# Second attention: one reciprocal for the row sums of two rounds, and block transposes four rounds behind their scores

## What is computed

```python
q = (q_c @ w_qb).reshape(b, s, NH, QK).transpose(0, 2, 1, 3)      # NH 32, QK 192
...
scores = jnp.einsum('bhqd,bhkd->bhqk', query, key_s) * scaling
attn = jax.nn.softmax(scores, axis=-1)
out = jnp.einsum('bhqk,bhkd->bhqd', attn, v)
out = out.transpose(0, 2, 1, 3).reshape(b, s, NH * VD)
return out @ w_o
```

## Time and profile before

| | |
|---|---|
| Median of 3 runs | 1026.47 us (1021.14 to 1027.76) |
| The profiled execution | 1023.77 us, its span 1021.9 us |
| Mean granted TensorE clock | 0.934 of full speed |
| The second attention | about 390 to 955 us of the span |
| TensorE busy | 849.0 us (83%) |
| VectorE busy | 764.2 us (75%) |
| ScalarE busy | 535.6 us (52%) |
| POOL busy | 520.7 us (51%) |
| Row maxima, L1351 | 256, 171.7 us; VectorE idle before them 36.1 us |
| Transposes, L1366 | 256, 178.6 us |

### The profile page before, as it was taken

How to read it: one execution, slowest core, us unless ns; L and a number is a source line. 1 busy time by engine, 2 the same in 40 slices (tenths; PEclk the granted TensorE clock), 3 DMA queues, 4 the chain that set the end, 5 groups by cost and what they waited for, 6 DMA issues and landing times. The chain is left out here.

```text
span 1021.9 us, 15116 instructions
## 1 busy us (share of the span) xinstructions
PE 849.0 (83%) x4552; PEld 563.1 (55%) x4552; DVE 764.2 (75%) x1588; ACT 535.6 (52%) x1142; POOL 520.7 (51%) x449
## 2 busy tenths in 40 slices
PE   5678886599978965799999999997999999985476
PEld 1667675477767743355555555564555555643145
DVE  1759998745535525999999999999999999982453
ACT  2267874623213743665666666564666665662143
POOL 2034342012110004888888888886888888872013
PEclk9979998599987986999999999998999999998779
DMA  9430000700023770455555555553555555555101
GB/s 328 159 129 2 1 2 1 276 23 1 1 82 126 246 227 0 111 132 126 130 130 129 128 132 131 126 131 93 129 128 132 128 130 129 127 130 118 56 11 72
DMA packets 73105, 112.29 MB, mean 110 GB/s; under 512 B 18816, under 2 KB 23936, under 8 KB 72768
## 3 DMA queue, kind: packets, MB, share of 16 engines
q1 hardware_dynamic: 60736, 94.54, 33.8%
q10 hardware_dynamic: 12288, 16.79, 6.9%
HBM read 42.06 MB, written 2.10 MB: 43 GB/s over the span
## 5 line engine op out<-in xcount | busy, mean ns | idle before, releaser
L1351 DVE TENSOR_REDUCE nmax<-bank 128x1 f32<-128x512 f32 x256 | 171.7, 671 | 36.1 <-PE bank L1291 35.9
L1429 ACT ACTIVATE prob<-bank,nmax 128x512 f32<-128x512 f32 x172 | 118.2, 687 | 132.9 <-DVE nmax L1351 132.1
L1488 POOL TENSOR_TENSOR prob<-prob,rinv 128x512 f32<-128x512 f32 x129 | 133.5, 1042 | 42.7 <-DVE rinv L1358 42.7
L1289 PE MATMUL bank<-xk_hi,q_hi 128*128 128x512 f32 x256 | 114.2, 446 | 28.0 <-ACT prob L1429 20.8
L1366 DVE STREAM_TRANSPOSE blk<-prob 128x512 f32<-128x512 f32 x172 | 120.0, 698 | 1.7 <-ACT prob L1444 0.4
L1289 PEld LDWEIGHTS bank<-xk_hi,q_hi 128*128 128x128 f32 x256 | 48.2, 188 | 108.8 <-issue 53.0
L1483 POOL TENSOR_TENSOR q_lo<-stage_a,q_hi 128x512 fp32r<-128x512 f32 x64 | 82.6, 1291 | 47.8 <-ACT q_hi L1423 47.8
L1290 PE MATMUL bank<-xk_lo,q_hi 128*128 128x512 f32 x256 | 101.5, 396 | 0.0
L1291 PE MATMUL bank<-xk_hi,q_lo 128*128 128x512 f32 x256 | 100.9, 394 | 0.0
L1429 ACT ACTIVATE stage_a<-bank,nmax 128x512 f32<-128x512 f32 x84 | 57.7, 687 | 56.4 <-DVE nmax L1351 56.0
L1479 POOL TENSOR_TENSOR stage_a<-stage_a 128x512 f32<-128x512 f32 x64 | 82.0, 1282 | 6.3 <-DVE stage_a L1346 6.3
(11 more groups left out here) (217 smaller groups left out, 2135.6 us busy)
## 6 DMA issues: line engine op xcount, KB each, us to landing
pT<-blk SPq DMA_DIRECT2D x384, 64.0 KB, 2.0
raw_e<-blk SPq DMA_DIRECT2D x384, 64.0 KB, 2.0
wmod<-in_wmod SPq DMA_DIRECT2D x12, 1024.0 KB, 12.0
raw_e<-in_wo SPq DMA_DIRECT2D x8, 1024.0 KB, 6.4
pT<-blk ACTq DMA_DIRECT2D x128, 64.0 KB, 2.1
raw_e<-blk ACTq DMA_DIRECT2D x128, 64.0 KB, 2.0
wqn<-in_wqn SPq DMA_DIRECT2D x8, 512.0 KB, 4.0
stage_a<-in_wqkv SPq DMA_DIRECT2D x4, 768.0 KB, 8.9
```

What stands on the lines that cost most here:

```text
L1289: pe.matmul(sbk, q_hi[:, u % 2, q], xk_hi[:, 2, ks], start=True, stop=False)
L1351: dve.tensor_reduce(nmax[:, s % RING:s % RING + 1], s_bank[s % 2][:, :], AX.X, ALU.max, negate=True).then_inc(max_done, 1)
L1429: act.activation(prob[s % RING], s_bank[s % 2][:, :], ACT.Exp, bias=nmax[:, s % RING:s % RING + 1], accum_out=rsum[:, s % RING:s % RING + ...
L1488: pool.tensor_tensor(prob[s % RING], prob[s % RING], bc(rinv[:, s % RING:s % RING + 1], [P, S]), ALU.mult).then_inc(norm_pool, 1)
```

## The change

The reciprocal is taken once in every two rounds, over two neighbouring columns of row sums, in even steps. POOL's scaling follows two rounds behind its scores instead of one, ScalarE's three instead of two, and the transpose four instead of three. `MOVE_LAG` is `TPB + TURN_LAG`, so ScalarE's moves go one step later too; SP's wait for the same count of transposes as before. Contexts and output projections keep their steps.

```diff
             ACT_NORM = 3
-            TURN_LAG = 3
+            TURN_LAG = 4
             MOVE_LAG = TPB + TURN_LAG
...
                     def row_inv(s):
-                        dve.wait_ge(exp_done, s + 1)
-                        if s >= RING:
-                            norm_ready(dve, s - RING)
-                        dve.reciprocal(rinv[:, s % RING:s % RING + 1], rsum[:, s % RING:s % RING + 1]).then_inc(rinv_done, 1)
+                        dve.wait_ge(exp_done, s + 2)
+                        for n in (s - RING, s + 1 - RING):
+                            if n >= 0:
+                                norm_ready(dve, n)
+                        dve.reciprocal(rinv[:, s % RING:s % RING + 2], rsum[:, s % RING:s % RING + 2]).then_inc(rinv_done, 1)
...
-                        if 1 <= s <= ROUNDS:
-                            row_inv(s - 1)
+                        if s % 2 == 0 and 2 <= s <= ROUNDS:
+                            row_inv(s - 2)
...
-                        ge(act, rinv_done, s - RING + 1)
+                        ge(act, rinv_done, (s - RING) // 2 + 1)
...
-                        if st == (ACT_NORM + 2) % TPB and 1 <= u <= UNITS:
-                            n = s - 2
-                            act.wait_ge(rinv_done, n + 1)
+                        if st == (ACT_NORM + 3) % TPB and 1 <= u <= UNITS:
+                            n = s - 3
+                            act.wait_ge(rinv_done, n // 2 + 1)
...
                     def normalize(s):
-                        pool.wait_ge(rinv_done, s + 1)
+                        pool.wait_ge(rinv_done, s // 2 + 1)
...
-                        if 1 <= s <= ROUNDS and (s - 1) % TPB != ACT_NORM:
-                            normalize(s - 1)
+                        if 2 <= s < ROUNDS + 2 and (s - 2) % TPB != ACT_NORM:
+                            normalize(s - 2)
```

## The result

The changed kernel takes 1040.03 us (median; 1038.14 to 1041.16) against 1025.62 us (1021.14 to 1027.76): a ratio of 1.0144, 95% interval 1.0106 to 1.0182. That is slower, beyond the noise but by less than 2%. The two intervals overlap at 1.0106 to 1.0126; the forecast was 1037 us.

What follows compares the result with a forecast made beforehand. VectorE, 93% busy, was taken to bound only two of four stretches, ScalarE and TensorE the others. Steady +9.8, first couple +1.05, tail +1.26, together +12.1 us, gave 1035.9 or 1038.6 by base; forecast 1037, range 1026 to 1048.

Steps and rivals of the forecast that it cites:

- Four stretches: One steady period of eight rounds (one couple of heads), 16.38 us, divided into four parts, each with its own limit.
- stretches 1 and 3: Row maximum of round 7 to round 2's, 5.27 us; subtraction cT_lo to round 6's maximum, 3.11; not set by VectorE.
- 2 and 4: Row maximum of round 2 to subtraction cT_lo, 5.25 us; maximum of round 6 to round 7's, 2.75; VectorE's own work.
- Reciprocals give 0 to 0.07 us a period: Of the reciprocals dropped in rounds 1, 3, 5 and 7, only round 3's shortens the period; taken as 0.05 us.
- Rival C: VectorE sets the whole period, so dropped reciprocals gain 0.51 us a period, 16 us in all: 1010 us; chance 0.07.
- The waits of the pair: New waits around the paired reciprocal, its scaling and the transpose cost nothing, covered by a round (2.05 us) or more.
- ScalarE's last move becomes the wait: Its last move goes to round 7, behind that round's exponential; context matmuls start 0.40 us later each period; chance 0.48.
- max 7: VectorE's row maximum of round 7 in a period of rounds 0 to 7; other numbers name their round likewise.
- SP has 0.5 us in hand: SP's last landing 10.7 us after round 3's maximum, matmul start 11.2 after it; the even unit eats 0.3 of that.
- Rival D: Collisions with ScalarE's issues stretch SP's twelve; matmul waits for SP, 0.3 to 0.5 us more a period: 1046 to 1052; chance 0.18.
- The first couple +1.05, the tail +1.26: SP's moves start 1.26 us later at both ends of the loop; at the first, some 0.2 of saved reciprocals comes off.
- What would show it: Signs: waits at L1302 nearly every period, some 12 us; period 16.7; idle before max 2 about 1.2, max 6 0.5.

Runs made afterwards that it cites:

- e7: Kernel before with two spare 128x1 reciprocals in each of rounds 1, 5 and 7, six more a period: 1025.47 us, ratio 0.9979.
- e8: Kernel before with two spare 128x1 reciprocals in each of rounds 2, 3, 4 and 6, eight more a period: 1041.71 us, ratio 1.0142.
- e1: Changed kernel with the transposes three rounds behind, as in the kernel before, keeping the paired reciprocals: 1026.68 us, ratio 0.9995.
- e9: The changed kernel measured once more, unaltered, in more rounds: 1037.53 us, ratio 1.0105.
- e3: Changed kernel with ScalarE's four moves of a unit issued one step earlier, SP's moves staying late: 1036.13 us, ratio 1.0107.
- e10: Kernel before with the first half of project_out behind the scores of round 6 instead of round 5: 1029.08 us, ratio 1.0021.

## Why the prediction was right

It named the mechanism, its place and its size. That the sum came out within 0.3 us of the traced 11.8 is in part luck: several terms are off and make up for one another. By its own steps:

- *Four stretches, of which VectorE sets only two.* Right. e7 and e8 show it from both sides: spare work in stretches 1 and 3 costs nothing, in 2 and 4 its full price.
- *Reciprocals give 0 to 0.07 us a period, taken as 0.05.* Right, 0.06 (5.19 instead of 5.25, in the changed kernel and in e1). But the price used for rounds 1 and 5, 0.19 us before a rotation, was wrong: it is 0.05 to 0.07, since most of that distance stays when the reciprocal goes. The sum didn't rest on it, as both rounds were covered. Rival C did: it was priced at 0.51 us a period (its own terms add up to 0.52). At 0.07 each it is an estimate of 0.28, 9 us instead of 16.
- *The waits of the pair cost nothing.* Right (e1).
- *ScalarE's last move becomes the wait, 0.40 us a period.* The chain is as written, each link a bit shorter: issue at max 7 + 0.69 (0.75 taken), 1.91 to landing, 0.14 to the matmul, together 2.74 in most periods (2.85 taken). The delay is thus 0.33, not 0.40. Six longer waits, which this term didn't hold, fill the gap: there the matmul is 0.4 to 1.2 us later than before, three times by SP's last move and three times by a slower landing. Stretch 1 grew by 0.38 us in the mean over 29 periods (5.53 to 5.91, with the first couple's and the output eviction's period in both).
- *SP has 0.5 us in hand.* Too generous as a statement for all periods. The even unit's moves take SP from 7.5 to 9.2 us where up to 8.7 was allowed for, and SP is last in three couples of the changed kernel besides the first, in six of e9. Rival D, as a small share on top of A rather than instead of it, is real. Its cause isn't: nothing shows that ScalarE's issues stretch SP's.
- *The first couple +1.05, the tail +1.26.* The fill came to +0.87, the tail to +0.56: SP started its last run later by 1.25 us, as expected, but its 48 moves took 0.7 us less than in the trace of before. No run shows that this is more than chance.
- *The sum +12.1 us.* 11.8 us in the trace, of which 0.9 in the eviction's period are not the change's as far as the runs tell; 14.8 and 10.8 by the two ratios. The range, 1026 to 1048, holds the time.
- *What would show it.* The waits at L1302 are in each period (10.7 us in 29 waits, 12 named), the period 16.65 (16.7 named), the idle before max 6 0.38 (0.5 named). The idle before max 2 is 0.92, not 1.2: the wait is shorter, and the reciprocals taken away left less room than priced. The last to be issued is ScalarE's, in 26 of the 29 couples behind the first.

The sentence taken from the Trainium skill, "DMA: Bandwidth & Descriptors", would have made the wait 0.6 us by its estimate of 2.15 us for 64 KB; the traces have 1.91 for the move that the matmul waits for. The page gives the formula in its section "Anatomy of one DMA" as a fit for transfers issued by GpSimd, while these are issued by SP and ScalarE, so it wasn't meant for them. The rule in the Trainium skill, "Perfetto Trace Analysis", section Optimizing Scalar/DVE Operations, about 60 ns an operation, fits what e8 measured (0.05 to 0.07 us). So does its condition that grouping pays if the engine is saturated: a mean of 93% busy didn't guarantee it, and e1 gained nothing measurable.

## What to carry to other kernels

Cut one period into stretches and ask of each which engine's wait ends last; an engine at 93% can be without influence in half of the period. When a step is moved, follow everything that is issued behind it and compare its new landing with the first use: here SP's moves began 1.25 us later, with 0.65 us to spare in the period read, and ScalarE's last move went from 2.01 us ahead of max 7 to 0.69 behind it, 2.7 us later with 2.3 to spare. One step of a loop isn't one time: it depends on which steps lie between. Queues with nearly equal slack hide one another, so a gain in one place can be paid back by the next: e3 took ScalarE's wait away and won 2.2 us, e10 shortened TensorE's stretch and won nothing, in large part because SP came next.

## What the runs showed of the hardware

- A 128x1 reciprocal on VectorE is 145 ns long in the profile, but one more of them delays the next instruction by only 0.05 to 0.07 us (e8). The distance between two starts around a removed instruction isn't its price.
- A 64 KB move between partitions of SBUF took 1.9 us from issue to landing at the least, 2.0 us in the median of 1024 moves, and over 2.4 us in 6 of 100, up to 3.7 (before and after; landings are matched to issues in their order). From the landing of the last one to the start of the waiting matmul it was 0.13 to 0.14 us each time.
- The issues of SP follow one another every 0.63 us in the median. One issue is 0.59 us long, but 50 of 768 in the kernel before are 0.78 us or more, up to 1.8. It isn't that ScalarE issues at the same moment: 18 of these 50 overlap an issue of ScalarE, against 371 of all 768. What stretches them wasn't tried.
